# Selective-scan stage of a layer: du and delta made ahead of the sums, skip term as a TensorE product

## The reference

```python
x_dbl = u @ w_x
dt, B, C = jnp.split(x_dbl, [DTR, DTR + N], axis=-1)
delta = jax.nn.softplus(dt @ w_dt)
deltaA = jnp.exp(delta[..., None] * A)
deltaBu = delta[..., None] * B[:, :, None, :] * u[..., None]
# h = deltaA * h + deltaBu, step by step over the sequence
y = jnp.einsum('bldn,bln->bld', hs, C) + u * D
return y * jax.nn.silu(res) @ w_out
```

## Time and profile before

| what | value |
|---|---|
| median of 3 runs | 2245.58 us |
| the profiled execution, its own time | 2248.75 us |
| its span | 2247.0 us |
| mean granted TensorE clock | 0.951 |
| busy in the span: PE, DVE, POOL, ACT | 90%, 65%, 53%, 38% |
| mixer_scan, from its first instruction to the first of experts | 1406.8 to 1873.9 us |
| first and last even scan (line 1067) begin | 1430.11 and 1866.36 us |

### The profile page before, as it was taken

How to read it: one execution, slowest core, us unless ns; L and a number is a source line. 1 busy time by engine, 2 the same in 40 slices (tenths; PEclk the granted TensorE clock), 3 DMA queues, 4 the chain that set the end, 5 groups by cost and what they waited for, 6 DMA issues and landing times. The chain is left out here.

```text
span 2247.0 us, 41708 instructions
## 1 busy us (share of the span) xinstructions
PE 2012.0 (90%) x15544; PEld 1429.2 (64%) x15544; DVE 1450.3 (65%) x1436; ACT 851.2 (38%) x1217; POOL 1196.6 (53%) x849
## 2 busy tenths in 40 slices
PE   6989999999999999999755699688888887899999
PEld 3867777777777777777543377355545553478874
DVE  5137666766766766666655471499989994736654
ACT  1124444444444444444322132455565551123320
POOL 3136666666666666666544400688878882312100
PEclk9999999999999999999855899799999998989999
DMA  4545555555555555554320400500030003001201
GB/s 171 155 138 172 168 168 167 168 168 166 169 170 167 166 163 174 167 171 140 119 69 30 166 19 1 122 1 1 8 106 1 1 0 122 35 0 52 66 4 38
DMA packets 180883, 229.71 MB, mean 102 GB/s; under 512 B 21232, under 2 KB 112112, under 8 KB 174416
## 3 DMA queue, kind: packets, MB, share of 16 engines
q1 hardware_dynamic: 180688, 227.04, 32.7%
HBM read 153.43 MB, written 73.53 MB: 101 GB/s over the span
## 5 line engine op out<-in xcount | busy, mean ns | idle before, releaser
L368 POOL TENSOR_TENSOR a_half<-a_pt 128x1024 f32<-128x1024 f32 x128 | 306.8, 2397 | 375.8 <-ACT a_pt L418 375.8
L418 ACT ACTIVATE a_pt<-a_shift 128x2048 f32<-128x2048 f32 x128 | 245.1, 1915 | 557.3 <-PE a_o L600 461.9
L487 DVE TENSOR_TENSOR a_shift<-a_s,a_neg_rows 128x2048 f32<-128x2048 f32 x128 | 293.3, 2292 | 195.9 <-ACT a_neg_rows L430 195.9
L474 DVE TENSOR_REDUCE a_top<-a_s 128x128 f32<-128x2048 f32 x128 | 293.1, 2290 | 74.8 <-PE a_s L575 74.8
L575 PE MATMUL a_s<-a_q_stack,a_stack 32*128 32x128 f32 x4096 | 163.9, 301 | 49.1 <-DVE a_shift L487 40.2
L966 POOL TENSOR_TENSOR s_odd_seen<-s_odd_state,s_c_row 128x512 f32<-128x512 f32 x128 | 162.5, 1269 | 79.7 <-DVE s_odd_state L1075 73.3
L534 PE MATMUL a_pj<-p_c_hi,p_wk_hi 128*128 128x512 f32 x448 | 198.5, 443 | 0.0
L575 PEld LDWEIGHTS a_s<-a_q_stack,a_stack 32*128 32x128 f32 x4096 | 138.6, 202 | 94.1 <-DVE a_shift L487 72.7
L1143 PE MATMUL s_ps<-s_even_seen,s_ident 128*128 128x512 f32 x256 | 140.4, 630 | 59.6 <-DVE s_even_seen L1084 59.5
L359 POOL TENSOR_TENSOR p_c_lo<-a_raw,p_c_hi 128x512 fp32r<-128x512 f32 x120 | 152.9, 1274 | 73.9 <-ACT p_c_hi L405 73.9
L1067 DVE TENSOR_TENSOR_SCAN s_ps<-s_ps,s_even_drive 128x512 f32<-128x512 f32 x128 | 156.4, 1222 | 54.0 <-ACT s_ps L1033 39.6
(11 more groups left out here) (204 smaller groups left out, 3858.8 us busy)
## 6 DMA issues: line engine op xcount, KB each, us to landing
kv_scratch<-a_k_new SPq DMA_DIRECT2D x128, 256.0 KB, 2.5
kv_scratch<-a_v_new SPq DMA_DIRECT2D x128, 256.0 KB, 3.7
a_stack<-kv_scratch SPq DMA_DIRECT2D x512, 64.0 KB, 2.3
a_v<-kv_scratch SPq DMA_DIRECT2D x32, 1024.0 KB, 6.2
a_raw<-in_ctx SPq DMA_DIRECT2D x120, 256.0 KB, 3.4
a_q_stack<-q_scratch SPq DMA_DIRECT2D x128, 64.0 KB, 2.2
s_c_row<-bc_scratch SPq DMA_DIRECT2D x32, 256.0 KB, 5.2
e_ew_raw<-in_ew SPq DMA_DIRECT2D x8, 1024.0 KB, 4.8
```

The lines of the kernel that those rows point to most:

```text
L368: nc.gpsimd.tensor_tensor(half[:], w[:, 0:2], w[:, 2:4], ALU.add).then_inc(halved, 1)
L418: nc.scalar.activation(pt_head(g, p), shift[:].rearrange("p (i n) -> p i n", n=BANK), ACT.Exp).then_inc(exped, 1)
L474: dve.tensor_reduce(top[:], s_ps[:].rearrange("p i n -> p (i n)").rearrange("p (k q) -> p q k", q=L), AX.X, ALU.max).then_inc(blocked, 1)
L487: dve.tensor_tensor(shift[:].rearrange("p (k q) -> p k q", q=L), s_ps[:].rearrange("p i n -> p (i n)").rearrange("p (k q) -> p k q", q=L), ...
```

## The change

In `mixer_in`, SyncE also loads `w_dt`, `a_log` and `d_skip`, sends B and C to `bc_scratch`, and waits for that; the identity and a buffer `rows` are allocated once and kept, `rows` being `wi_raw`, then `b_row`, then `w_out`, then `h_t`. In `mixer_scan`, delta, du and two of the eight diagonals are made by VectorE before tile 0, the other six by ScalarE in tile 0. `turn_du` and `make_delta` stand ahead of the sums of k = 4 and k = 5. `exp_delta` moves from k = 1 to k = 7. `u * D` is a product of TensorE with `skip_diag` that opens each sum, and `close` reads the sum from PSUM. `w_out` is loaded during the last tile. In `experts` the two first loads and TensorE's wait for them go.

```diff
@@ mixer_in, sync
-                    sp.dma_start(ident[:], ident_dram).then_inc(a_in, 16)
+                    sp.dma_start(ident[:], to_load[0]).then_inc(a_in, 16)
...
-                    for dst, src in ((bi, b_in), (wc, w_conv), (bc, b_conv), (wx, w_x)):
+                    for dst, src in ((bi, b_in), (wc, w_conv), (bc, b_conv), (wx, w_x)) + to_load[1]:
...
+            sp.wait_ge(xd_out, G)
+            sp.dma_start(bc_scratch, xd[DTR:XD, :]).then_inc(a_in, 16)
+            sp.wait_ge(a_in, 64)
@@ mixer_scan, sync
-            sp.dma_start(bc_scratch, xd[DTR:XD, :]).then_inc(bc_out, 16)
-            for dst, src in ((wd[0:DTR, :], w_dt), (a_neg[:], a_log), (dsk[:], d_skip), (ident[:], ident_dram)):
-                sp.dma_start(dst, src).then_inc(w_in, 16)
-            sp.wait_ge(bc_out, 16)
...
+            for k in range(PAIRS):
+                sp.wait_ge(even_driven, PAIRS * (TILES - 1) + k + 1)
+                sp.dma_start(rows[:, k, :], w_out[:, k, :]).then_inc(w_out_in, 16)
+            sp.wait_ge(w_out_in, 16 * PAIRS)
@@ mixer_scan, gpsimd
-            pool.wait_ge(w_in, 64)
-            pool.wait_ge(b_turned_out, 1)
-            for k in range(PAIRS):
-                nc.gpsimd.tensor_tensor(diag[:, k], ident[:].unsqueeze(1).to_broadcast([P, BG, L]),
-                                        b_turned[:, 0:BG, 2 * k + 1].unsqueeze(2).to_broadcast([P, BG, L]),
-                                        ALU.mult).then_inc(diag_out, 1)
-            add_delta(0)
-            make_du(0)
...
-                if k == 2 and t + 1 < TILES:
+                if k == 2 and 1 <= t < TILES - 1:
                     add_delta(t + 1)
-                if k == 3 and t + 1 < TILES:
+                if k == 3 and 1 <= t < TILES - 1:
                     make_du(t + 1)
@@ mixer_scan, scalar
+            def make_skip(d):
+                nc.scalar.activation(skip_diag[:, d], ident[:], ACT.Copy, scale=dsk[:, d:d + 1]).then_inc(skip_diag_out, 1)
...
-            for step in (empty_delta, exp_delta, log_delta):
-                for t in range(2):
-                    step(t)
+            for t in range(2):
+                size_delta(t)
+                exp_delta(t)
+            for t in range(2):
+                log_delta(t)
...
+            act.wait_ge(b_turned_out, 1)
...
                 if q == 0:
                     empty_du(0)
+                    make_skip(0)
+                if t == 0 and k + EARLY < PAIRS:
+                    make_diagonal(k + EARLY, 0)
                 if k == 1 and 1 <= t < TILES - 1:
-                    exp_delta(t + 1)
                     log_delta(t + 1)
-                if k == 6 and t + 1 < TILES:
+                if k == 5 and t + 1 < TILES:
                     empty_du(t + 1)
                 if k == 7 and t + 2 < TILES:
-                    empty_delta(t + 2)
+                    size_delta(t + 2)
+                    relu_delta(t + 2)
+                    exp_delta(t + 2)
+                if k == 6 and t + 1 < DT:
+                    make_skip(t + 1)
@@ mixer_scan, vector
+            def first_delta(t):
+                dve.wait_ge(soft_out, log_no(t))
+                dve.scalar_tensor_tensor(out=delta[:, t], in0=y_ps[:, t, :], scalar=0.0, in1=delta[:, t], op0=ALU.max,
+                                         op1=ALU.add).then_inc(delta_out, 1)
+
+            def first_du(t):
+                dve.wait_ge(delta_out, t + 1)
+                dve.tensor_tensor(du[:, t], delta[:, t], u[:, t, cols_of(t)], ALU.mult).then_inc(du_out, 1)
+
+            def first_diagonal(k):
+                dve.tensor_tensor(diag[:, k], ident[:].unsqueeze(1).to_broadcast([P, BG, L]),
+                                  b_turned[:, 0:BG, 2 * k + 1].unsqueeze(2).to_broadcast([P, BG, L]),
+                                  ALU.mult).then_inc(early_diag, 1)
+
+            dve.wait_ge(b_turned_out, 1)
+            first_diagonal(0)
+            first_delta(0)
+            first_du(0)
+            first_diagonal(1)
+            first_delta(1)
+            first_du(1)
...
-            def finish(t):
+            def close(t):
                 d = t % DT
                 dve.wait_ge(summed, odd_sum_no(PAIRS * (t + 1) - 1))
-                dve.scalar_tensor_tensor(out=u[:, d, cols_of(t)], in0=u[:, d, cols_of(t)], scalar=dsk[:, d:d + 1],
-                                         in1=y_ps[:, t % 2, :], op0=ALU.mult, op1=ALU.add).then_inc(skipped, 1)
-
-            def close(t):
-                d = t % DT
-                dve.wait_ge(skipped, t + 1)
-                dve.tensor_tensor(u[:, d, cols_of(t)], u[:, d, cols_of(t)], gate[:, d, cols_of(t)], ALU.mult)
+                dve.tensor_tensor(u[:, d, cols_of(t)], y_ps[:, t % 2, :], gate[:, d, cols_of(t)], ALU.mult)\
+                   .then_inc(closed, 1)
...
                 if k == 2 and t >= 1:
-                    finish(t - 1)
-                if k == 3 and t >= 1:
                     close(t - 1)
-            finish(TILES - 1)
             close(TILES - 1)
@@ mixer_scan, tensor
             def add_even(t, k, q):
                 if k == 0:
-                    pe.wait_ge(soft_out, relu_no(min(t + 1, TILES - 1)))
+                    if t:
+                        pe.wait_ge(soft_out, exp_no(min(t + 1, TILES - 1)))
                     pe.wait_ge(du_t_out, t + 1)
+                    pe.wait_ge(skip_diag_out, min(t, DT - 1) + 1)
+                    pe.matmul(y_ps[:, t % 2, :], skip_diag[:, t % DT], u[:, t % DT, cols_of(t)], start=True, stop=False)
...
             for t, k, q in steps:
                 if q + 1 < len(steps):
                     drive_odd(*steps[q + 1])
+                if k == 4 and t + 1 < TILES:
+                    turn_du(t + 1)
+                if k == 5 and t + 2 < TILES:
+                    pe.wait_ge(du_t_out, t + 2)
+                    make_delta(t + 2, (t + 1) % 2)
                 add_even(t, k, q)
                 if q >= 1:
                     add_odd(*steps[q - 1])
-                if k == 4 and t + 1 < TILES:
-                    turn_du(t + 1)
-                if k == 6 and t + 2 < TILES:
-                    pe.wait_ge(du_t_out, t + 2)
-                    make_delta(t + 2, (t + 1) % 2)
@@ experts
-            sp.dma_start(wo[:], w["w_out"]).then_inc(first_in, 16)
-            sp.dma_start(ident[:], ident_dram).then_inc(first_in, 16)
...
-            pe.wait_ge(first_in, 32)
```

More of the change, by code:

```diff
@@ L666, with mixer_in @@
 G, BG = 2, B // 2
-def mixer_in(nc, a_scratch, x, wo_t, bo, w_in, b_in, w_conv, b_conv, w_x, ident_dram, xres, u, gate, xd):
+def mixer_in(nc, a_scratch, x, wo_t, bo, w_in, b_in, w_conv, b_conv, w_x, ident, to_load, bc_scratch, rows, xres, u, gate, xd):
     with ExitStack() as ctx:
@@ L755, in _ @@
             round_x(B - 1)
-            act.wait_ge(w_in_s, 64)
+            act.wait_ge(w_in_s, 112)
             act.wait_ge(padded, 1)
@@ L864, in _, with mixer_scan @@
                     x_dbl()
-def mixer_scan(nc, w_dt, a_log, d_skip, ident_dram, bc_scratch, u, gate, xd):
+def mixer_scan(nc, wd, a_neg, dsk, ident, bc_scratch, w_out, rows, u, gate, xd):
     with ExitStack() as ctx:
         st = Stage(nc, ctx, "s")
[L876 to L879, removed]
         PAIRS = N // 2
         TILES = G * DT
-        b_row = st.sb("b_row", [P, PAIRS, BANK])
+        b_row = rows
         c_row = st.sb("c_row", [P, N, BANK])
@@ L1131, in drive_odd @@
                     pe.wait_ge(odd_scanned, q - 1)
-                pe.wait_ge(diag_out, k + 1 if t < DT else PAIRS + BG * (k + 1))
+                if t < DT and k < EARLY:
+                    pe.wait_ge(early_diag, k + 1)
+                else:
+                    pe.wait_ge(diag_out, diag_no(k) if t < DT else diag_no(PAIRS - 1) + BG * (k + 1))
                 for b in range(BG):
@@ L1176, with experts @@
 K3 = 3
-def experts(nc, w, ident_dram, iota, xres, u, out):
+def experts(nc, w, ident, iota, rows, xres, u, out):
     with ExitStack() as ctx:
         st = Stage(nc, ctx, "e")
-        ident = st.sb("ident", [P, P])
         ones = st.sb("ones", [P, P])
         with ExitStack() as early:
-            wo, pw = (Stage(nc, early, "e").sb(name, shape) for name, shape in (("w_out", [P, DT, D]),
-                                                                               ("pw", [P, KC, D])))
+            pw = Stage(nc, early, "e").sb("pw", [P, KC, D])
+        wo = rows
         x1_lo = st.sb("x1_lo", [P, KC, T], F32R)
@@ L1195, in experts @@
         x1_t = st.sb("x1T", [P, KC, T])
-        h_t = st.sb("hT", [P, KC, T])
+        h_t = rows[:].rearrange("p c d -> p (c d)").rearrange("p (k t) -> p k t", k=KC)
         rms = st.sb("rms", [P, G, BANK])
@@ L1602, in layer @@
         u = st.sb("u", [P, DT, T])
-        with nc.sbuf_tensor("l_gate", [P, DT, T], F32) as gate, nc.sbuf_tensor("l_xd", [P, T], F32) as xd:
+        ident = st.sb("ident", [P, P])
+        rows = st.sb("rows", [P, DT, D])
+        with ExitStack() as mixer:
+            sm = Stage(nc, mixer, "l")
```

(9 more changed lines are left out.)

56 lines of the change are left out of this document (28 added, 28 removed).

## The result

| what | before | after |
|---|---|---|
| median (lowest to highest), 4 runs each | 2246.18 (2243.32 to 2246.79) | 2173.92 (2173.56 to 2174.24) |
| the profiled execution, its own time | 2248.75 | 2174.16 |
| first even scan, after the stage's first VectorE instruction | 23.04 | 10.87 |
| tile 0 | 27.69 | 25.14 |
| tiles 1 to 15, first scan of tile 1 to last even scan | 408.56 | 363.08 |

The ratio of the medians is 0.9682, with a 95% interval from 0.9667 to 0.9698: faster by 72.3 us, where 78 were forecast; 2173.9 lies in the range. The two profiled executions are 74.6 us apart, their spans 75.0. Five rows of the table carry 73.1 of these 75.0 (the head 12.2, tile 0 2.55, the tiles 45.5, the crossing to experts 12.3, the last row 0.7); in the other 1.9 the stage began earlier, behind code that is almost all the same.

A forecast was written before the change was run, and what follows sets the result against it. No engine fills the scan; beside eight steps, 4.96 us a tile go to `finish`, `close` and waits, plus the stage's edges. Gains 49.3 + 16.2 + 0.8 + 11.7 = 78.0 from 2248.75 give 2170.8 profiled, 2168 median; range 2154 to 2186.

The forecast's parts named there:

- ScalarE's lateness at the tile's edge: Tiles: with delta made earlier, VectorE's 2.0 us wait before a tile's first scan and 0.7 in steps 0 to 2 go.
- `close` from PSUM: Tiles, VectorE: reading PSUM and one SBUF tensor, `close` has a pitch of 0.58 us, not 1.52.
- GpSimd's 0.86 us at k = 5: Tiles: GpSimd's `add_delta` and `make_du` at k = 2 and 3 make the scan of k = 5 0.86 us late.
- The step that failed: Tiles, TensorE: 23.3 us of work fits into 24.0; sums 0.7 late at the edge reach no scan.
- the forecast tile: One steady tile of the scan: 22.56 + 0.58 + 0.04 + 0.86 = 24.04 us, bounds 23.3 and 25.2.
- the 78.0: Whole kernel: total forecast gain in us, 49.3 (tiles) + 16.2 (head) + 0.8 (end) + 11.7 (experts).
- The crossing of tiles 7 and 8: Second diagonals, log and table loads on ScalarE make its decay for k = 2 of tile 8 2.4 us late (1 to 5).
- The head: Up to tile 1's first scan: earlier first scan, rows of B and C costing 1.5 us; gain 16.2 us (12 to 19).
- The end and experts: Scan's tail gains 0.8 us without `finish`; experts gain 11.7 (8.6 to 11.8), TensorE starting at once and first products faster.
- TensorE as the bound: Rival, chance 0.14: TensorE's surpluses add up in the scan, 25.2 us a tile, 2184 us in all.
- the forecast's 0.7 us to spare a tile: Tiles: TensorE's 23.3 us of work leave 0.7 us to spare in a tile of 24.0.
- The clock did not fall: Rival, chance 0.03: TensorE's clock drops in the scan, making it slower than before; sixteen tiles at 1.2 GHz give about 2530.

The follow-up runs named there:

- undo_order: Changed kernel with `turn_du` and `make_delta` back behind the sums of k = 4 and k = 6, `empty_du` at k = 6: 2204.41 us against 2173.92.
- undo_exp: Changed kernel with `exp_delta` back from k = 7 to k = 1: 2171.76 us against 2173.92.
- undo_skip: Changed kernel with `finish` and the old `close` back on VectorE in place of TensorE's skip product: 2185.93 us against 2173.92.
- no_skip: Changed kernel without the term u × D, so without TensorE's skip product and ScalarE's `skip_diag`: 2169.58 us against 2173.92.
- skip_k2: Changed kernel with the skip product moved from the sum of k = 0 to that of k = 2: 2167.22 us against 2173.92.
- skip_twice: Changed kernel with the skip product made twice, a second one behind the first: 2182.65 us against 2173.92.
- undo_w_out: Changed kernel with `w_out` loaded at the start of experts again, TensorE waiting for it: 2183.35 us against 2173.92.

## Why the prediction was right, and where it was off

- **ScalarE's lateness at the tile's edge: right.** Its wait for delta went from 4.46 to 0.40 us, VectorE's 2.0 and the 0.7 behind it are gone, and undo_order brings back the first two (5.00 and 2.52). That these waits really came from the order is thereby shown, not only read. The 0.7 in steps 0 to 2 comes back in neither undo_order (0.15 in tile 3) nor undo_exp: each of the two moves alone is enough to remove it.
- **`close` from PSUM: right.** Fifteen last 678 ns in the mean (0.60 by pitch), against 1.59 with both inputs in SBUF, and undo_skip's last 1602. The operation is the same and GpSimd works beside it in both; an input lies elsewhere. The kernel before has the counter-test, its last `close`, with both inputs in SBUF and nothing running on GpSimd:

```profile
1872.97 0.69 DVE L1096 TENSOR_TENSOR l_u<-l_u,l_gate 128x512 f32<-128x512 f32 x1
```

It takes 0.69 us, not 1.59, so two SBUF inputs alone do not make it slow. The Trainium skill, page "SBUF — State Buffer", section "Who interferes with whom", says that a VectorE instruction contends with GpSimd when it has two SBUF inputs and, outside its 2-port modes, not when it has at most one; these runs agree.
- **GpSimd's 0.86 us at k = 5: right,** in place and size (0.78 shown as idle, 0.86 by pitch). undo_skip shows that `finish` and the slow `close` had covered it.
- **The step that failed** is that of TensorE: "the skip product makes the sums some 0.7 us late at the edge, made up at 0.2 us a step, while `drive_odd` can be 1.0 us late before a scan waits". The lateness was sized well enough, and `drive_odd` did hold. But I followed only that one reader of TensorE. GpSimd's weighing waits for the sum of two steps before, and it queues ahead of `add_delta` and the drives; through it 0.31 us a tile came out at k = 4. no_skip and skip_k2 give 24.02, the forecast tile; the changed kernel has 24.33. Over fourteen tiles 0.29 more than forecast make 4.1 us. It is the largest miss of the sum: the tiles gave 3.8 less than forecast, the head 1.5 less, experts 0.2 less, 5.5 in all. The medians differ by 5.7 less than the 78.0, the profiled executions by only 3.4 less. That this is less than 5.5 is luck: 1.9 us of the stage's earlier start and 0.7 in the last stretch stand in no term of the forecast.
- **The crossing of tiles 7 and 8: right in place and kind.** ScalarE's decay was 2.07 us late at the scan of k = 2 of tile 8 (1619.48), and tile 8 with it 26.25 against 24.33, 1.9 us more where 2.4 were forecast. Tiles 1 to 15 gave 45.5 of the forecast 49.3.
- **The head: right in sum, partly by luck.** The first scan came 10.87 us after VectorE's first instruction; the forecast's 10.6 counts from the stage's first instruction of all, 0.27 us earlier, and by that count it is 11.1. But VectorE's products there cost 0.69 and not 1.6, for GpSimd was still waiting for rows, and then VectorE waited 1.92 for that very drive: I had the rows late only at the end of tile 0, and they were late from the first. Head and tile 0 together gained 14.7, forecast 16.2.
- **The end and experts: right in sum.** 0.8 and 11.5 us came, forecast 0.8 and 11.7; the last two pieces of `w_out` landed in 2.7 us each. Against the kernel before both terms hold too: the pause of TensorE went from 10.51 to 1.05, 9.46 less with the 0.8 of `finish` in it, so 8.7 where 8.6 were forecast, and the first products took 2.8 less where 3.1 were. Undoing the load alone costs 9.4, of which the slow clock is 1.65; the identity's load was not put back there.
- **The rivals.** TensorE as the bound is false for this kernel: skip_k2 keeps its work and has the tile of no_skip. It is not far off, as 0.86 us more at the tile's edge is paid in full in skip_twice. That the forecast's 0.7 us to spare a tile is right as an amount no run contradicts and none shows. The clock did not fall: 1.00 over 363 us. The clock swing between short groups that cycle PSUM banks, of which the Trainium skill tells on the page "TensorE: Matmul & The Clock Gate", section "A second HAM failure mode: psum-queue depth-cycling", again has no trace here.
- **How the parts add up.** Undone alone they cost 30.5 (order), 12.0 (skip), 9.4 (`w_out`) and 0 (`exp_delta`), 51.9 of 72.3 us. The rest, 20.4, is the head and tile 0, where 14.7 were gained, the wait and the load of the identity, and what the parts do to each other: GpSimd's lateness is hidden by `finish` and `close` or not at all, so the skip part is worth less behind the new order than its instructions say. The head's parts were not undone one by one.

## What to carry to other kernels

When work is put into an engine's queue, follow every reader of what it delays, also through an engine that is far from full: here 0.86 us on TensorE reached VectorE by way of GpSimd, which was waiting for a sum, and the same product two steps later cost nothing that the tile shows. A short instruction on the bounding engine can be another's cover: taking it away is worth less than its length. And before an extra is moved on an in-order queue, count from the scan to the end of that queue's next drive, for the slack that one place has (0.60 us under `close`) can be missing at every other.

## What was unexpected of the hardware

The first 32 products of experts took 16.78 us behind a pause of 10.51 us on TensorE in the kernel before, 15.62 behind 9.09 in undo_w_out, and 13.97 behind 1.05 in the changed kernel: after pauses of nearly the same length the loss was 2.8 us in one program and 1.65 in another. The granted clock of these stretches accounts for both. TensorE worked without a gap from its first product on; in the kernel before 0.50 was granted for the first 5.5 us (1882.66 to 1888.16), in undo_w_out for the first 3.3 (1816.68 to 1819.98), and 1.00 soon after. At half speed a stretch loses half its length: 2.75 and 1.65 us, an estimate from these times. The changed kernel, with 1.05 us of pause, had 1.00 throughout.

And stretches with the same code differ by up to 5 us between programs that are alike otherwise: the last 350 us of the kernel took 350.2 in skip_k2 and 355.4 in no_skip. This too goes with the clock. In the 60 us that begin 50 us behind the first add of experts, 0.86 was granted in skip_k2 and 0.77 in no_skip. There the same 64 products (line 1525, 1519 in no_skip) took 29.55 and 30.65 us behind pauses of 4.47 and 4.46, and the 64 short ones after them 10.76 and 12.86 behind 1.50 and 1.51: 3.2 of the 5.2 us. Why the clock came back at different times after equal pauses no run here shows; with such a spread only the stretches that an edit touches can be compared to tenths.
